# Attention in a decoder layer: which engine copies the spread reciprocals out of PSUM

## The chip, the cores and the metric

The kernel runs on one core of a Trainium2 chip. Five engines work side by side and meet at semaphores: TensorE (PE), VectorE (DVE), ScalarE (ACT), GpSimd (POOL) and SyncE (SP, which issues the DMAs). Each takes its instructions strictly in the order in which they are written. The metric is the device time of one execution in microseconds, median of three runs: 1494.46 us before the change (1493.82 to 1495.74).

## The reference

A pre-norm decoder layer: self-attention, cross-attention and a feed-forward block, each added to x. The change lies in the self-attention, and of it the reference computes:

```python
q = (x @ Wq).reshape(B, T, H, Dh)          # B 4, T 512, H 16, Dh 32
k = (x @ Wk).reshape(B, T, H, Dh)
v = (x @ Wv).reshape(B, T, H, Dh)
scores = jnp.einsum('bthd,bshd->bhts', q, k)
mask = jnp.tril(jnp.ones((T, T), dtype=scores.dtype))
scores = scores * mask
attn = jax.nn.softmax(scores / T ** 0.5, axis=-1)
out = jnp.einsum('bhts,bshd->bthd', attn, v).reshape(B, T, H * Dh)
return out @ Wo
```

The mask multiplies, so tokens beyond the diagonal keep a score of zero and still count in the softmax.

## The kernel before

The four batches (n) are walked one after the other; each has an attention stage of about 62 us, and between two stages stand the projections, the cross-attention and the norms, in which PE is nearly always busy. After the fourth stage comes the feed-forward block (from about 545 us).

An attention stage has 16 units u. A unit is a row tile of 128 queries (i = u % 4, so 128, 256, 384 or 512 tokens wide) of one group of four heads (hg = u // 4); its four rows j are the heads. "Row (u, j)" is the place in the loops that all engines share. In row (u, j):

- PE issues `scores` of the unit after (u+1, j) and then `turn` (u, j), the transposes of the probabilities into a PSUM bank. At j = 3 it also issues `recips(u-1)`, which spreads the reciprocals of a unit's denominators over 32 columns a head by a matmul with the identity, and `values(u-1)`, the product with V. At (4, 1), (8, 1), (12, 1) it issues `repack`, twelve transposes of packed feed-forward weights.
- ACT issues `exp` (u, j), and copies three of the four turned heads to SBUF (`turned`, L1223). At j = 1 it issued `recip_out(u-2)`, L1229: the spread reciprocals from PSUM into `r_den`. At (4, 3), (8, 3), (12, 3) it issues `repacked`, the copy of the first half of the packed weights (L1243).
- DVE works one unit ahead of `exp`: it issues `row_max` (the row maxima, L1548), at j = 3 the copy of the fourth turned head (`turned`, L1558), and at (u, 0), behind its `row_max`, `divide(u-3)`, L1586: the values in bank 6 times `r_den` into `o_sum`. The second half of the packed weights is its copy too (L1599).
- POOL turns each row maximum into the exp's bias (`shift`, L682), masks values (L692), converts packed weights (L675) and for head groups 0 to 2 takes the low part of the output (`out_tail`, L698), which the next group's first `divide` waits for (`o_lo`).

All turned heads, the spread reciprocals and the packed weights go through a ring of three PSUM banks (4, 5, 7). Slot s may be written when slot s-3 has been read, and `turn_read` says who reads that:

```python
def turn_read(n, slot):
    for u in range(UNITS):
        if slot == recip_slot(u):
            return rden_out, n * UNITS + u + 1
```

Three slots behind the spread reciprocals of unit u stands the third turned head of unit u+2 (`turn(u+2, 2)`), for u = 2, 6 and 10 the first half of `repack`, and for u = 14 the spread reciprocals of unit 15. Each has this wait on `rden_out`, the semaphore that the copy into `r_den` raises:

```python
def turn(n, u, j):
    if slot >= 3:
        pe.wait_ge(*turn_read(n, slot - 3))
def repack(n, r):
    for half in range(2):
        pe.wait_ge(*turn_read(n, pack_slot(r, half) - 3))
def recips(n, u):
    pe.wait_ge(*turn_read(n, slot - 3))
```

At the end of a stage ACT and DVE copy the next batch's normed x (L1186, L1533) before the last two units are divided.

Of the kernel before, what the change touches and what calls it, by code (L numbers as in the profile page):

```python
# [46 lines left out]
P = 128  # L47
# [8 lines left out]
UNITS = HG * TT  # L56
# [35 lines left out]
def decoder_layer(nc, x, ctx_1024, Wq, Wk, Wv, Wo, xWq, xbq, xWk, xbk, gate_p, gate_s, up_p, up_s, down_p, down_s, out):  # L92
    with ExitStack() as ctx:
        def sem(name):
            return ctx.enter_context(nc.semaphore(name))
# [26 lines left out]
        def sb(name, shape, dt):  # L122
            return first.enter_context(nc.sbuf_tensor(name, shape, dt))
# [26 lines left out]
        r_den = sb("r_den", [P, 2, P], F32)  # L150
# [87 lines left out]
        pt_act, pt_dve, av_done, o_done, o_hi, o_lo = (sem(n) for n in ("pt_act", "pt_dve", "av_done", "o_done", "o_hi", "o_lo"))  # L238
        den_done, rcol_done, r_full, rden_out = (sem(n) for n in ("den_done", "rcol_done", "r_full", "rden_out"))
# [18 lines left out]
        ROWS = 4 * UNITS  # L258
        wide = [(i + 1) * P for i in range(TT)]

        def turn_slot(h):


            return h + 2 * (max(0, h - 2) // 16) + max(0, h // 4 - 1)

        def pack_slot(r, half):
            return (turn_slot(16 * r + 17) + 1 if r < HG - 1 else recip_slot(UNITS - 2) + 1) + half

        def recip_slot(u):
            return turn_slot(4 * u + 7) + 1 if u < UNITS - 1 else pack_slot(HG - 1, 1) + 1  # L270

        def turn_bank(slot):
            return bank[(4, 5, 7)[slot % 3]]
# [14 lines left out]

        AT_RECIP, AT_DIVIDE = 9, 12
        AT_SUMS, AT_TURNED, AT_RECIPROCALS = 1, 3, 2
        AT_OUT = 0

# [887 lines left out]
        def _(act):  # L1182
            def spread_heads(st, n, banks):
                for k in range(KT):
                    act.wait_ge(spread_full[st], n * KT + k + 1)
                    nc.scalar.activation(spread_to(st, n, 0, k), bank[banks + k][:], ACT.Copy, scale=XF if st == 2 else XS).then_inc(spread_hi[st], 1)  # L1186
# [15 lines left out]
            def exp(n, u, j):  # L1202
                i = u % TT
                act.wait_ge(shift_done, n * ROWS + 4 * u + j + 1)
                if u >= 2:
                    act.wait_ge(t_full, n * ROWS + 4 * (u - 2) + j + 1)
                nc.scalar.activation(prob[:, u % 2, j, 0:wide[i]], bank[j][:, 0:wide[i]], ACT.Exp,  # L1207
                                     bias=nmx[:, u % 2, j:j + 1], accum_out=den[:, u % 2, j:j + 1]).then_inc(exp_done, 1)

            def exp_zero(n, u):  # L1210

                if u >= 2:
                    act.wait_ge(den_done, beyond_units(n, u - 2))
                    act.wait_ge(v_zero_done, beyond_units(n, u - 2))
                act.wait_ge(shift_done, n * ROWS + 4 * u + 4)
                nc.scalar.activation(e_zero[:, u % 2, :], nmx[:, u % 2, :], ACT.Exp).then_inc(e_zero_done, 1)

            def turned(n, u, j):
                i = u % TT
                act.wait_ge(t_full, n * ROWS + 4 * u + j + 1)  # L1220
                if u >= 2:
                    act.wait_ge(av_done, n * UNITS + u - 1)
                nc.scalar.copy(prob_t[:, u % 2, j, 0:wide[i]], turn_bank(turn_slot(4 * u + j))[:, 0:wide[i]]).then_inc(pt_act, 1)  # L1223

            def recip_out(n, u):
                act.wait_ge(r_full, n * UNITS + u + 1)
                if u >= 2:
                    act.wait_ge(o_done, n * UNITS + u - 1)
                nc.scalar.copy(r_den[:, u % 2, :], turn_bank(recip_slot(u))[:, 0:P]).then_inc(rden_out, 1)  # L1229

            def out_head(n, hg):
                act.wait_ge(o_done, n * UNITS + 4 * hg + 4)
                if hg == 0:
                    act.wait_ge(xf_stored, n * 16 + 16)
                nc.scalar.copy(o_t[:, 0, hg, :], o_sum[:]).then_inc(o_hi, 1)

            def repacked(n, r):
                nb = n * (NB // B) + r
                act.wait_ge(pk_full, 2 * nb + 1)
                act.wait_ge(sd_stored, 16 * NB)  # L1240
                if r > 0:
                    act.wait_ge(pk_stored, 32 * nb)
                nc.scalar.copy(pk_t[:, 0], turn_bank(pack_slot(r, 0))[:].bitcast(F16)[:, 0:HALF]).then_inc(pk_out0, 1)  # L1243
# [188 lines left out]
            def body(n, last):  # L1432
                for u in range(UNITS):
                    for j in range(4):
                        if u == 1 and j == 0:
                            act.wait_ge(att_full, n * KT + KT)
                        if u > 0:
                            exp(n, u, j)
                        if j == 3 and u % TT < TT - 1:
                            exp_zero(n, u)  # L1440
                        if j == AT_OUT and u % TT == 2 and u > TT:
                            out_head(n, u // TT - 1)

                        if j >= 2:
                            turned(n, u, j - 2)
                        elif j == 0 and u > 0:
                            turned(n, u - 1, 2)
                        if j == 3 and u % TT == 0 and u > 0:
                            repacked(n, u // TT - 1)
                        h = 4 * u + j - AT_RECIP  # L1450
                        if h >= 0 and h % 4 == 0:
                            recip_out(n, h // 4)
                turned(n, UNITS - 1, 2)
                if not last:
                    spread_heads(0, n + 1, 0)
                for u in range((ROWS - 1 - AT_RECIP) // 4 + 1, UNITS - 1):
                    recip_out(n, u)
                repacked(n, HG - 1)
                recip_out(n, UNITS - 1)
                out_head(n, HG - 1)  # L1460
                between(n, True, not last)

            walk(body)(act)


# [24 lines left out]
        def _(dve):  # L1490
# [87 lines left out]
            def divide(n, u):  # L1578

                hg, i = u // TT, u % TT  # L1580
                if i == 0 and hg > 0:
                    dve.wait_ge(o_hi, n * HG + hg)
                    dve.wait_ge(o_lo, n * HG + hg)
                dve.wait_ge(rden_out, n * UNITS + u + 1)
                dve.wait_ge(av_done, n * UNITS + u + 1)
                nc.vector.scalar_tensor_tensor(o_sum[:, P * i:P * i + P], bank[6][:, P * (u % 2):P * (u % 2) + P], QS, r_den[:, u % 2, :],  # L1586
                                               ALU.mult, ALU.mult).then_inc(o_done, 1)
# [296 lines left out]
            def body(n, last):  # L1884
# [27 lines left out]
                if not last:  # L1912
                    spread_tails(0, n + 1, 0)
                divide(n, UNITS - 2)
                repacked(n, HG - 1)
                divide(n, UNITS - 1)
# [63 lines left out]
```

## Time and profile before

| | us |
|---|---|
| median of 3 runs | 1494.46 |
| lowest, highest | 1493.82, 1495.74 |
| the profiled execution's own time | 1495.65 |
| its span, first to last instruction | 1493.9 |
| busy in the span: PE, DVE, ACT, POOL | 1429.5, 991.0, 723.6, 379.6 |

The span is 1.75 us shorter than the execution's own time. Busy time is summed over stages that have different limits. Instructions of one engine overlap in the rows: one starts while the last still writes, so the start of the next less the start of this is the time that it takes in the queue, and its duration is the time until its result is there. A number in square brackets at the end of a row is the idle time of the engine just before it, with what ended it.

### The profile page before, as it was taken

The page shows a single profiled execution, that of the slowest core. Times are in us where ns is not written, and L with a number is a line of the kernel's source. Part 1 is how long each engine was busy: PE and PEld are TensorE (multiplying, and loading weights), DVE is VectorE, ACT ScalarE, POOL GpSimd, SP SyncE. Part 2 cuts the span into 40 slices and gives each one's busy share as a digit, 9 for nine tenths or more (in the row PEclk, how much of TensorE's full clock was granted, in tenths as well). Part 3 has the DMA queues.
Part 4 walks back from the last instruction along what each step waited for, and adds up shares of the span by engine and source line. Part 5 has one row for each costly group of instructions (what it writes and reads, how often), then busy time and mean ns, then how long its engine had stood idle before and what let it go on. Part 6 is the DMA issues. An engine that isn't in the chain of part 4 may idle for free.

```text
span 1493.9 us, 26821 instructions
## 1 busy us (share of the span) xinstructions
PE 1429.5 (96%) x8896; PEld 722.3 (48%) x8896; DVE 991.0 (66%) x2113; ACT 723.6 (48%) x1676; POOL 379.6 (25%) x688
## 2 busy tenths in 40 slices
PE   6989999999988799999999999999999999999999
PEld 4465456456545554444444444444444444444444
DVE  7785787578567858877666656755766666666533
ACT  5795289249616855353353353343442533533532
POOL 0051024004371865522112111112212212212100
PEclk9999999999999999999999999999999999999999
DMA  7553423341444431011001001001001000000011
GB/s 246 145 154 107 127 75 101 93 117 66 160 138 124 143 112 45 1 32 32 17 17 32 17 17 32 16 17 34 17 16 32 17 16 30 16 20 1 1 57 57
DMA packets 72765, 93.29 MB, mean 62 GB/s; under 512 B 6064, under 2 KB 57008, under 8 KB 72240
## 3 DMA queue, kind: packets, MB, share of 16 engines
q1 hardware_dynamic: 72624, 91.51, 19.9%
q8 instruction: 76, 1.25, 0.3%
q14 instruction: 65, 0.53, 0.1%
HBM read 66.59 MB, written 24.90 MB: 61 GB/s over the span
## 4 chain that ended last, share of the span: by engine, by line
PE 79%; DVE 7%; ACT 6%; issue 6%; POOL 2%; DMA 0%; ACTq 0%; DVEq 0%; POOLq 0%; SPq 0%
PE bank L829 23%; PE bank L830 23%; PE bank L831 23%; ACT prob L1207 3%; PE bank L893 2%; PE bank L914 2%; PE bank L842 1%; PE bank L954 1%; PE bank L969 1%; PE bank L882 1%; ACT prob_t L1223 1%; PE bank L964 1%; PE bank L923 1%; DVE G L1665 1%; DVE c L1690 1%
## 5 line engine op out<-in xcount | busy, mean ns | idle before, releaser
L829 PE MATMUL bank<-xs,G 128*128 128x512 f16 x896 | 339.8, 379 | 2.6 <-ACT c L1295 1.2
L831 PE MATMUL bank<-xs,G 128*128 128x512 f16 x896 | 339.6, 379 | 0.0
L830 PE MATMUL bank<-xs,G 128*128 128x512 f16 x896 | 339.6, 379 | 0.0
L1295 ACT COPY c<-bank 128x512 f32<-128x512 f32 x192 | 111.2, 579 | 219.1 <-PE bank L831 214.3
L1676 DVE TENSOR_TENSOR c<-bank,c 128x512 f32<-128x512 f32 x128 | 88.0, 689 | 192.8 <-PE bank L831 192.8
L829 PE MATMUL bank<-Wd,hid 128*128 128x512 f16 x512 | 194.1, 379 | 2.8 <-DVE X L1730 2.8
L830 PE MATMUL bank<-Wd,hid 128*128 128x512 f16 x512 | 194.0, 379 | 0.0
L831 PE MATMUL bank<-Wd,hid 128*128 128x512 f16 x512 | 194.0, 379 | 0.0
L667 POOL TENSOR_TENSOR c<-c,m 128x512 f32<-128x512 f32 x64 | 82.1, 1284 | 386.3 <-ACT c L1295 386.3
L1730 DVE SCALAR_TENSOR_TENSOR X<-bank,col,X 128x512 f32<-128x512 f32 x128 | 95.4, 749 | 101.5 <-PE bank L831 101.4
L1548 DVE CUSTOM_DVE_ANT_0 bank<-bank,mask,col 128x128 f32<-128x128 f32 (+3 forms) x256 | 139.2, 549 | 26.0 <-issue 13.9
L1207 ACT ACTIVATE prob<-bank,nmx 128x128 f32<-128x128 f32 (+3 forms) x256 | 147.4, 579 | 10.3 <-POOL nmx L682 9.7
L829 PEld LDWEIGHTS bank<-xs,G 128*128 128x128 f16 x896 | 87.6, 98 | 114.9 <-ACT c L1295 7.3
L831 PEld LDWEIGHTS bank<-xs,G 128*128 128x128 f16 x896 | 87.7, 98 | 105.7
L830 PEld LDWEIGHTS bank<-xs,G 128*128 128x128 f16 x896 | 87.7, 98 | 102.5
L682 POOL TENSOR_TENSOR nmx<-zero,mx 128x1 f32<-128x1 f32 x256 | 52.8, 207 | 316.8 <-DVE mx L1548 296.9
L893 PE MATMUL bank<-ident,prob 128*128 128x128 f32 x640 | 112.0, 277 | 16.9 <-DVE prob_t L1558 4.9
L1318 ACT CAST hid<-c 128x512 f16<-128x512 f32 x128 | 79.2, 619 | 91.6 <-DVE c L1690 88.1
L1310 ACT ACTIVATE c<-c,col 128x512 f32<-128x512 f32 x96 | 69.4, 723 | 94.8 <-DVE c L1676 94.8
L1696 DVE TENSOR_TENSOR hid<-c,hid 128x512 f16<-128x512 f32 x128 | 86.1, 712 | 27.0 <-ACT hid L1318 27.0
L633 POOL TENSOR_TENSOR w_sum<-w_full 128x384 f32<-128x384 f32 (+1 forms) x32 | 23.6, 737 | 313.9 <-DVE w_full L1657 313.8
L1223 ACT COPY prob_t<-bank 128x128 f32<-128x128 f32 (+2 forms) x192 | 89.2, 465 | 8.4 <-PE bank L893 8.4
(182 smaller groups left out, 2406.3 us busy)
## 6 DMA issues: line engine op xcount, KB each, us to landing
stack<-qk_dram SPq DMA_DIRECT2D x128, 128.0 KB, 3.3
sc_in<-scale_t SPq DMA_DIRECT2D x32, 384.0 KB
qk_dram<-qk SPq DMA_DIRECT2D x32, 256.0 KB, 2.7
packed_t<-pk_t SPq DMA_DIRECT2D x32, 192.0 KB, 2.0
pk_in<-packed_t SPq DMA_DIRECT2D x32, 192.0 KB
X<-in_x_dram SPq DMA_DIRECT2D x4, 1024.0 KB, 5.8
pk_in<-L_ffn_gate_W_packed_dram SPq DMA_DIRECT2D x16, 256.0 KB, 2.7
pk_in<-n_L_ffn_up_W_packed_dram SPq DMA_DIRECT2D x16, 256.0 KB, 3.0
```

The source lines that it names most:

```text
L667: nc.gpsimd.tensor_tensor(c22[x][:], c22[x][:], m5[x][:], ALU.add).then_inc(c22_out, 1)
L829: pe.matmul(o, lhs(0), rhs(0), start=first, stop=False, skip_group_check=onto)
L830: pe.matmul(o, lhs(0), rhs(1), start=False, stop=False, skip_group_check=onto)
L831: return pe.matmul(o, lhs(1), rhs(0), start=False, stop=stop, skip_group_check=onto)
L893: mm = pe.transpose(turn_bank(slot)[:, P * k:P * k + P], prob[:, u % 2, j, P * k:P * k + P], ident[:])
L1207: nc.scalar.activation(prob[:, u % 2, j, 0:wide[i]], bank[j][:, 0:wide[i]], ACT.Exp, bias=nmx[:, u % 2, j:j + 1], accum_out=den[:, u % 2, ...
L1223: nc.scalar.copy(prob_t[:, u % 2, j, 0:wide[i]], turn_bank(turn_slot(4 * u + j))[:, 0:wide[i]]).then_inc(pt_act, 1)
L1295: nc.scalar.copy(dst[:], bank[BANK_Y if which == M5 else x][:]).then_inc(c_copied, 1)
L1548: nc.vector.tensor_tensor_reduce(out=bank[j][:, 0:wide[i]], in0=bank[j][:, 0:wide[i]], in1=mask[:, P * (3 - i):P * (3 - i) + wide[i]], sca ...
L1676: nc.vector.tensor_tensor(dst[:], bank[at][:], dst[:], ALU.add).then_inc(comb, 1)
L1696: nc.vector.tensor_tensor(hid[:, beta, q, r, 1, :], quarter(1, idx)[:], hid[:, beta, q, r, 0, :], ALU.subtract).then_inc(hid_lo, 1)
L1730: nc.vector.scalar_tensor_tensor(xv, bank[4 + t][:], C_OUT, xv, ALU.mult, ALU.add).then_inc(acc_out, 1)
```

## The change

`recip_out` is taken out of ACT's program. DVE issues the same copy at the head of `divide(n, u)`, behind a wait for `r_full` (the spread reciprocals are in the bank), and raises `rden_out` with it. The multiplication behind it still waits for `rden_out`, now raised by DVE itself.

```diff
-        AT_RECIP, AT_DIVIDE = 9, 12
+        AT_DIVIDE = 12
...
-            def recip_out(n, u):
-                act.wait_ge(r_full, n * UNITS + u + 1)
-                if u >= 2:
-                    act.wait_ge(o_done, n * UNITS + u - 1)
-                nc.scalar.copy(r_den[:, u % 2, :], turn_bank(recip_slot(u))[:, 0:P]).then_inc(rden_out, 1)
...
-                        h = 4 * u + j - AT_RECIP
-                        if h >= 0 and h % 4 == 0:
-                            recip_out(n, h // 4)
...
-                for u in range((ROWS - 1 - AT_RECIP) // 4 + 1, UNITS - 1):
-                    recip_out(n, u)
                 repacked(n, HG - 1)
-                recip_out(n, UNITS - 1)
...
             def divide(n, u):
 
                 hg, i = u // TT, u % TT
+                dve.wait_ge(r_full, n * UNITS + u + 1)
+                nc.vector.tensor_copy(r_den[:, u % 2, :], turn_bank(recip_slot(u))[:, 0:P]).then_inc(rden_out, 1)
                 if i == 0 and hg > 0:
                     dve.wait_ge(o_hi, n * HG + hg)
                     dve.wait_ge(o_lo, n * HG + hg)
                 dve.wait_ge(rden_out, n * UNITS + u + 1)
```

There are 64 such copies, 16 in each attention stage. The instructions of PE, POOL and SP keep their order.

DVE, row (5, 0) of a stage, where the unit divided is 2 and the bank is the one that `repack` takes next. Before:

```order
L1548 ISA bank0,mx<-bank0,mask,col 128x256 [waits shift_done,s_full]
L1548 ISA mx 128x1
L1586 SCALAR_TENSOR_TENSOR o_sum<-bank6,r_den 128x128 [waits av_done,rden_out]
L1599 CAST pk_t<-bank5 128x768 [waits sd_stored,pk_full]
L1548 ISA bank1,mx<-bank1,mask,col 128x256 [waits shift_done,s_full]
```

and now (lines of the changed file):

```order
L1536 ISA bank0,mx<-bank0,mask,col 128x256 [waits shift_done,s_full]
L1536 ISA mx 128x1
L1570 COPY r_den<-bank4 128x128 [waits r_full]
L1576 SCALAR_TENSOR_TENSOR o_sum<-bank6,r_den 128x128 [waits av_done,rden_out]
L1589 CAST pk_t<-bank5 128x768 [waits sd_stored,pk_full]
L1536 ISA bank1,mx<-bank1,mask,col 128x256 [waits shift_done,s_full]
```

The copy stands behind the row maxima of (5, 0), and the multiplication and everything after it one instruction further back. On ACT the same copy stood at row (4, 1), as here before the change:

```order
L1207 ACTIVATE prob,den<-bank1,nmx 128x128 [waits t_full,shift_done]
L1229 COPY r_den<-bank4 128x128 [waits o_done,r_full]
L1207 ACTIVATE prob,den<-bank2,nmx 128x128 [waits t_full,shift_done]
L1223 COPY prob_t<-bank5 128x128 [waits av_done,t_full]
L1207 ACTIVATE prob,den<-bank3,nmx 128x128 [waits t_full,shift_done]
```

It moved from between two exponentials of unit 4 to three rows later in the common order, on the other engine.

PE at rows (4, 0) to (4, 3), the same before and now; bank 4 is the first that `repack` writes:

```order
L882 MATMUL bank0<-stack 128x256 [waits exp_done]
L893 MATMUL bank5<-ident,prob 128x128 [waits pt_act,exp_done]
L882 MATMUL bank1<-stack 128x256 [waits exp_done]
L893 MATMUL bank7<-ident,prob 128x128 [waits pt_dve,exp_done]
L989 MATMUL bank4<-ident16,pk_16 128x128 [waits rden_out,pk_conv]
L989 MATMUL bank4<-ident16,pk_16 128x128 x5
L989 MATMUL bank5<-ident16,pk_16 128x128 [waits pt_act]
L989 MATMUL bank5<-ident16,pk_16 128x128 x5
L882 MATMUL bank2<-stack 128x256 [waits exp_done]
L893 MATMUL bank7<-ident,prob 128x128 [waits pt_act,exp_done]
L882 MATMUL bank3<-stack 128x256 [waits exp_done]
L893 MATMUL bank4<-ident,prob 128x128 [waits pk_out0,exp_done]
```

The first row, into bank 0, is the product whose row maxima DVE takes in row (5, 0). What moved is not PE's order but who raises `rden_out` for its fifth row, and behind what.

## Rows read from the trace of the kernel before

**Rows 1.** Page, its span and part 1: busy us (share) x instructions.

```profile
span 1493.9 us, 26821 instructions
...
PE 1429.5 (96%) x8896; PEld 722.3 (48%) x8896; DVE 991.0 (66%) x2113; ACT 723.6 (48%) x1676; POOL 379.6 (25%) x688
```

**Rows 2.** Windows: length; PE, PEld, DVE, ACT, POOL busy; clock; DMA share; GB/s.

```profile
72.00:134.00 62.00, 55.74 (x824) 40.61 (x825) 48.77 (x187) 57.72 (x205) 26.89 (x97) 1.00 0.52 152
134.00:204.00 70.00, 68.58 (x328) 34.62 (x325) 45.34 (x122) 21.63 (x51) 1.23 (x7) 1.00 0.37 106
...
475.00:545.00 70.00, 56.42 (x806) 39.63 (x807) 53.59 (x194) 56.82 (x200) 47.30 (x116) 0.98 0.44 141
```

**Rows 3.** Groups by line: the copy that moves; busy, mean ns, idle before.

```profile
L1229 ACT COPY r_den<-bank 128x128 f32<-128x128 f32 x64 | 19.6, 306 | 0.4 <-PE bank L923 0.2
```

**Rows 4.** Timeline of ACT, first stage: start us, us, instruction, idle before.

```profile
99.91 0.82 ACT L1243 CAST pk_t<-bank 128x768 int16<-128x768 f16 x1
...
105.91 0.29 ACT L1229 COPY r_den<-bank 128x128 f32<-128x128 f32 x1
106.05 0.63 ACT L1207 ACTIVATE prob<-bank,nmx 128x384 f32<-128x384 f32 x1
...
109.10 0.72 ACT L1207 ACTIVATE prob<-bank,nmx 128x512 f32<-128x512 f32 x1
```

**Rows 5.** Timeline of DVE, first stage, rows (9, 0) to (10, 1).

```profile
99.60 0.29 DVE L1586 SCALAR_TENSOR_TENSOR o_sum<-bank,r_den 128x128 f32<-128x128 f32 x1
100.04 0.56 DVE L1599 CAST pk_t<-bank 128x768 int16<-128x768 f16 x1 [0.16 <-PE bank L989]
...
101.86 0.29 DVE L1558 COPY prob_t<-bank 128x128 f32<-128x128 f32 x1
...
103.40 0.29 DVE L1586 SCALAR_TENSOR_TENSOR o_sum<-bank,r_den 128x128 f32<-128x128 f32 x1
103.60 0.62 DVE L1548 CUSTOM_DVE_ANT_0 bank<-bank,mask,col 128x384 f32<-128x384 f32 x1
```

**Rows 6.** Timeline of DVE in a norm: each waits for the one before.

```profile
422.00 0.46 DVE L1516 SCALAR_TENSOR_TENSOR rs<-rs,var 128x4 f32<-128x4 f32 x1
422.49 0.17 DVE L1518 SCALAR_TENSOR_TENSOR rs<-rs 128x4 f32<-128x4 f32 x1
```

**Rows 7.** Timeline of PE, first stage: the second repack, and three turned heads that wait.

```profile
99.17 0.83 PE L989 MATMUL bank<-ident,pk 128*128 128x128 f16 x12
...
100.87 0.30 PE L893 MATMUL bank<-ident,prob 128*128 128x128 f32 x1 [0.29 <-ACT pk_t L1243]
...
103.27 0.38 PE L893 MATMUL bank<-ident,prob 128*128 128x128 f32 x2
...
110.84 0.63 PE L893 MATMUL bank<-ident,prob 128*128 128x128 f32 x4 [0.64 <-ACT prob L1207]
```

**Rows 8.** Timeline of POOL, units 10 and 11 of the first stage.

```profile
104.35 0.44 POOL L682 TENSOR_TENSOR nmx<-zero,mx 128x1 f32<-128x1 f32 x1 [0.55 <-DVE mx L1548]
...
106.51 1.16 POOL L698 TENSOR_TENSOR o_t<-o_sum,o_t 128x512 f16<-128x512 f32 x1
...
108.88 0.19 POOL L682 TENSOR_TENSOR nmx<-zero,mx 128x1 f32<-128x1 f32 x1 [1.07 <-DVE mx L1548]
```

**Rows 9.** Timeline of DVE, unit 11 of the first stage.

```profile
107.75 0.29 DVE L1586 SCALAR_TENSOR_TENSOR o_sum<-bank,r_den 128x128 f32<-128x128 f32 x1 [0.81 <-issue]
...
110.14 0.55 DVE L1558 COPY prob_t<-bank 128x384 f32<-128x384 f32 x1
```

**Rows 10.** Timeline of DVE, end of the first stage.

```profile
131.78 0.28 DVE L1586 SCALAR_TENSOR_TENSOR o_sum<-bank,r_den 128x128 f32<-128x128 f32 x1
```

**Rows 11.** Timeline of PE, end of the first stage.

```profile
132.21 1.08 PE L914 MATMUL bank<-prob_t,V 128*32 128x128 f32 x32 [0.69 <-DVE o_sum L1586]
```

**Rows 12.** Timeline of DVE in the last stage.

```profile
480.38 0.36 DVE L1640 TENSOR_SCALAR bits<-pk_in 128x384 uint32<-128x384 uint32 x1 [1.37 <-DMA sc_in<-scale_t]
```

**Rows 13.** Timeline of POOL in the last stage.

```profile
487.12 1.66 POOL L622 TENSOR_TENSOR w_full<-codes,sc_in 128x768 f32<-128x768 f16 x1
```

## The prediction

> **What bounds the kernel now.** I read the page first, then the busy time by stage, then the groups by line, and last the timelines of all engines side by side through one period of four units. The page gives PE 1429.5 us of a span of 1493.9 [rows 1], so the kernel is bound by PE as a whole; but the change touches the four attention stages alone, and there it looks otherwise. In a window of 62 us over the first stage ACT is busy 57.72 us, PE 55.74, DVE 48.77; the 70 us behind it have PE at 68.58 and ACT at 21.63 [rows 2]. So ACT is the fullest engine in attention, and whatever delay PE leaves a stage with is not made up behind it. The last stage carries feed-forward work too: DVE 53.59 and ACT 56.82 of 70 us [rows 2].
>
> The copy that moves takes 19.6 us in 64 pieces, 306 ns each [rows 3]. Its price in ACT's queue is smaller: it starts at 105.91 and the next exponential at 106.05, 0.14 us [rows 4].
>
> **What is removed.** 64 x 0.14 = 9.0 us of ACT's queue, 2.2 us a stage. It is worth time only where ACT is what the others wait for.
>
> **What is added on DVE.** The trace has a DVE copy of this very size out of PSUM: 0.29 us [rows 5]. The multiplication behind it now waits for its result. In a norm, where each instruction waits for the one before, one of 0.46 us starts at 422.00 and the next at 422.49, 0.03 us after its end [rows 6]. So each copy pushes what is behind it on DVE by 0.29 + 0.03 = 0.32 us: 20.5 us in all, 5.1 a stage, against 62 - 48.8 = 13.2 us in which DVE is free. Ends: 0.20, the time in the queue of a multiplication of this size with no wait behind it (103.40 to 103.60 [rows 5]), and 0.46, the longest small instruction of rows 6. I take 0.32.
>
> The multiplication that nothing waits behind lets the next start 0.09 us before its own end [rows 5], the one that is waited for 0.03 us after its end [rows 6]: the wait costs 0.12 us. The Trainium skill, "VectorE: DVE Perf Modes", section "The DRAIN you can't avoid", says of chained copies that a semaphore after each costs nothing extra. By that rule the copy would cost 0.20 and the sum below would be 17 x 0.12 = 2.0 us less; the rows here say otherwise.
>
> **What the later copy holds up.** This is the part that the diff does not show. `rden_out` does not only release the multiplication; it also frees the bank that PE writes three slots later. Before, ACT read it at row (u+2, 1). Now DVE reads it at row (u+3, 0), behind the row maxima of the unit u+3, and these wait for scores that PE issues only just ahead of the instruction that needs the bank.
>
> For u = 2, 6, 10 that instruction is the first transpose of `repack`. In the second period it starts at 99.17 [rows 7], with DVE's multiplication at 99.60 [rows 5]. The copy takes that place, ends at 99.89, and PE goes on 0.15 us after DVE's end (DVE's copy starts at 110.14 and takes 0.55, PE starts at 110.84 [rows 7, 9]): 100.04. The bank is 0.87 us late. Behind it queue on PE the rest of the repack, the scores of (9, 2) and (9, 3), the turned heads, the spread and the values; on ACT the copy of packed weights, at 99.91 [rows 4]; on DVE the other, at 100.04, which already waited for PE by 0.16 [rows 5]. PE's turned head (8, 3) already waited 0.29 for ACT's copy [rows 7]. The first half of a repack takes about 0.5 us of the 0.83, so ACT's copy had some 0.2 us to spare. That leaves 0.65 us of each, three times a stage. Ends: 0 (all absorbed) and 0.87.
>
> In the other units it is a transpose (u+2, 2). For u = 7 DVE's multiplication stands at 103.40 and PE's transpose (9, 2) at 103.27 [rows 5, 7]: 103.40 + 0.29 + 0.15 = 103.84, 0.57 us late, and much the same where u % 4 is 0. But PE waits for ACT soon after, and the copies of turned heads on ACT come later still; I take nothing. For u % 4 = 1 the copy stands in front of the wait below. Ends: 0, and 0.5 us for each of 8 a stage.
>
> **Where 0.32 us lies on the path.** From row (10, 0) on, DVE works without a gap into the row maxima that POOL waits for: 104.35, idle 0.55 for DVE. POOL then runs through to the low part of the output, 106.51 plus 1.16 us, and DVE stands 0.81 us until it is done and divides at 107.75 [rows 8, 9]. From there DVE runs through again; POOL waits for its maximum, 108.88 plus 0.19, and ACT's exponential starts at 109.10, 0.03 us after it; PE's transpose at 110.84 starts 0.15 us after DVE's copy ends [rows 4, 7, 8, 9]. So DVE, POOL, DVE is a chain with no slack, as long as ACT's own. The copy at row (10, 0) lengthens it by 0.32. The copy at (11, 0) does not: it stands in front of the 0.81 us of waiting. This chain is there in rows (6, 0), (10, 0) and (14, 0) to (u+1, 0): three times a stage. At the end of a stage DVE copies the normed x, divides at 131.78, and PE, idle 0.69 us, starts the last values 0.15 us after it, at 132.21 [rows 10, 11]; the copy adds 0.32 in front.
>
> **The sum.** A stage: 3 x 0.65 + 3 x 0.32 + 0.32 = 3.2 us. Where DVE's chain is as long as ACT's, ACT's gain is lost in waiting; in the first four units, without that chain, two copies are saved: 2 x 0.14 = 0.3. That makes 2.9 us, and 8.8 in three stages. In the last stage DVE is behind a DMA until 480.38 and runs without a gap until POOL starts the weights at 487.12 [rows 12, 13], with two copies in between, 0.64; after that POOL leads for a while. Three more copies are on the chain, 0.96, and one of the three repacks is late by 0.7 with nothing to absorb it; the others wait for ACT or POOL anyway. The end of that stage has no normed x and hides its copy. Together 2.3. In all 8.8 + 2.3 = 11.1 us. On the profiled execution's own 1495.65 us that makes 1506.8; the median of the runs is 1.2 lower, so I predict 1505.6.
>
> **Rivals.**
> *ACT's relief wins.* ACT is the fullest engine [rows 2], DVE has the room, and 0.14 us leave ACT 64 times: 9.0 us, 1485.5. It needs all DVE delays to fall into DVE's gaps and PE to get its banks in time; the transpose at 110.84 and the exponential at 109.10 speak against it [rows 4, 7], since both follow DVE. The Trainium skill, "Perfetto Trace Analysis", section "Optimizing Scalar/DVE Operations", says that work may be moved between the two when one is saturated, which read this way round speaks for the change; it also gives DVE the larger access overhead on PSUM, which agrees with 0.20 against 0.14 us in the queue [rows 4, 5].
> *DVE's time alone.* The late bank is absorbed by the waits of 0.29 and 0.16 us and by ACT's queue. A stage: 0.96 + 0.32 - 0.3 = 1.0; the last 1.6; in all 4.6: 1499.1.
> *All of it hides*, gain and loss cancel: 1494.5.
> *The late transposes count too.* From the point where the three-bank ring is the limit, nothing absorbs them: 8 a stage at up to 0.5 us, some 3 us a stage net, 12 more than the forecast: 1518.
>
> **How the numbers follow.** A change under 0.2%, 3 us, cannot be told from none by a measurement of this kernel. Chances: forecast 0.57, DVE's time alone 0.15, late transposes 0.12, all hides 0.08, ACT's relief 0.08. The two bounds of the copy (0.20 and 0.46) move the sum by -2.0 and +2.4 us over its 17 places, the ends of the repack term move it by -6.5 and +2.2 over its ten. The range that holds 8 in 10 goes from 1498, with the case of DVE's time alone, to 1513. Faster 0.08, same 0.09, slower 0.83.
>
> **What would show it.** In the profile after: the DVE copy into `r_den` at 0.28 to 0.30 us and the multiplication 0.03 us behind it; before each `repack` PE idle by 0.5 us or more, put down to DVE; the periods from one repack to the next longer by about 1.0 us; the DVE busy time up by 18 us, ACT's down by 20. The stretches between the attention stages and the feed-forward block keep their length. I am wrong if PE does not wait at the repack, if the copy stands in a gap of DVE in the rows (u, 0) with u % 4 = 2, or if the attention stages grow shorter.

## The result: 0.6% slower, and the profile after

The changed kernel takes 1503.80 us (median of 4 runs, 1502.88 to 1506.35), the kernel before 1494.93 us (4 runs on the same chip). The ratio is 1.0062, with a 95% interval from 1.0046 to 1.0077, so the loss of 8.9 us is real. The profiled execution of the changed kernel took 1503.5 us, against 1495.65 before.

The page of the kernel after, its span and part 1, which answer to [rows 1]:

```profile
span 1501.8 us, 26765 instructions
...
PE 1428.0 (95%) x8896; PEld 720.2 (48%) x8896; DVE 1003.7 (67%) x2177; ACT 718.1 (48%) x1612; POOL 379.0 (25%) x688
```

PE does the same work in the same time; the span is 7.9 us longer, and all of this is idle PE. The windows of the kernel after say where (length; busy of PE, PEld, DVE, ACT, POOL; clock; DMA share; GB/s), the same first two stretches as [rows 2]:

```profile
72.00:134.00 62.00, 53.32 (x780) 38.66 (x780) 50.33 (x198) 55.99 (x188) 26.88 (x98) 1.00 0.51 150
134.00:204.00 70.00, 68.39 (x357) 34.77 (x358) 45.18 (x121) 20.14 (x44) 0.76 (x4) 1.00 0.38 111
```

In 62 us of the first attention stage PE is busy 2.4 us less than before, and ACT, which lost its copies, is now idle for 6.0 us instead of 4.3. Nobody was waiting for the time that ACT was given.

The groups by line of the kernel after (busy, mean ns of one, idle before them and its releasers): the copy in its new place, and the first repack instructions.

```profile
L1570 DVE COPY r_den<-bank 128x128 f32<-128x128 f32 x64 | 18.3, 286 | 0.0
...
L989 PE MATMUL bank<-ident,pk 128*128 128x128 f16 x192 | 13.7, 219 | 8.7 <-DVE r_den L1570 7.6 <-ACT prob_t L1223 1.2
```

PE waits 7.6 us at the repacks for the copy that DVE now makes. The list of waits of the kernel after (engine, line, releaser: us in all, times, longest) counts them, and shows the other place:

```profile
PE bank L989 <- DVE r_den L1570: 7.6, 11, 0.7
...
PE bank L923 <- DVE r_den L1570: 2.9, 3, 1.0
```

Eleven repacks of the twelve with u = 2, 6, 10 wait, and the three stages that end in a norm wait once more at their end. One such repack on all engines, second period of the first stage, timelines of the kernel after (start us, us, instruction, idle before). It answers to [rows 4, 5, 7]. DVE:

```profile
100.23 0.14 DVE L1536 DVE_READ_ACCUMULATOR2_ANT mx<- 128x1 f32 x1
100.23 0.29 DVE L1570 COPY r_den<-bank 128x128 f32<-128x128 f32 x1
100.55 0.29 DVE L1576 SCALAR_TENSOR_TENSOR o_sum<-bank,r_den 128x128 f32<-128x128 f32 x1
101.53 0.56 DVE L1589 CAST pk_t<-bank 128x768 int16<-128x768 f16 x1 [0.69 <-PE bank L989]
```

PE, and behind it ACT:

```profile
100.66 0.83 PE L989 MATMUL bank<-ident,pk 128*128 128x128 f16 x12 [0.70 <-DVE r_den L1570]
```

```profile
101.19 0.80 ACT L1237 CAST pk_t<-bank 128x768 int16<-128x768 f16 x1 [0.54 <-PE bank L989]
```

The copy ends at 100.52 and PE starts 0.14 us later, after 0.70 us of idling. ACT then waits 0.54 us for PE, and DVE 0.69 instead of 0.16: the lateness of one 0.29 us instruction reaches three engines.

Starts of the first repack instruction in the first stage: 84.05, 99.17, 114.29, 130.31 before; 84.61, 100.66, 116.72, 132.92 after. A period of four units, 15.12 us before, takes 16.05. The last values of the stage move from 132.21 [rows 11] to 135.14, those of the second stage from 264.17 to 270.02, those of the third from 396.09 to 404.87: 2.93, 2.92 and 2.93 us a stage.

### The profile page after: what moved, and what is told of

It is laid out like the page before. It is cut to its first block, busy times and chain, and to the rows that moved or that the text cites. A ratio compares the mean times of both kernels' runs of the same rounds, so it can differ in the third digit from the quotient of the medians.

```text
span 1501.8 us, 26765 instructions
## 1 busy us (share of the span) xinstructions
PE 1428.0 (95%) x8896; PEld 720.2 (48%) x8896; DVE 1003.7 (67%) x2177; ACT 718.1 (48%) x1612; POOL 379.0 (25%) x688
## 3 DMA queue, kind: packets, MB, share of 16 engines
q8 instruction: 76, 1.25, 0.4%
## 4 chain that ended last, share of the span: by engine, by line
PE 81%; issue 7%; DVE 5%; ACT 3%; POOL 3%; DMA 0%; POOLq 0%; ACTq 0%; DVEq 0%; SPq 0%
PE bank L829 24%; PE bank L831 24%; PE bank L830 24%; PE bank L893 2%; ACT prob L1207 2%; PE bank L914 2%; POOL nmx L682 1%; PE bank L842 1%; PE bank L954 1%; PE bank L969 1%; PE bank L964 1%; POOL pk L675 1%; PE bank L882 1%; ACT prob_t L1223 1%; POOL v_zero L692 1%
## 5 line engine op out<-in xcount | busy, mean ns | idle before, releaser
L1536 DVE CUSTOM_DVE_ANT_0 bank<-bank,mask,col 128x128 f32<-128x128 f32 (+3 forms) x256 | 139.2, 550 | 21.2 <-issue 13.2
L1207 ACT ACTIVATE prob<-bank,nmx 128x128 f32<-128x128 f32 (+3 forms) x256 | 140.2, 557 | 15.6 <-POOL nmx L682 13.4
L893 PEld LDWEIGHTS bank<-ident,prob 128*128 128x128 f32 x640 | 74.4, 140 | 50.9 <-ACT prob L1207 25.6
```

The source lines that it names most:

```text
L893: mm = pe.transpose(turn_bank(slot)[:, P * k:P * k + P], prob[:, u % 2, j, P * k:P * k + P], ident[:])
L1536: nc.vector.tensor_tensor_reduce(out=bank[j][:, 0:wide[i]], in0=bank[j][:, 0:wide[i]], in1=mask[:, P * (3 - i):P * (3 - i) + wide[i]], sca ...
```

## The experiments

All times are medians; each ratio is to the kernel before, run on the same chip (its median there was 1495.28 us beside early_all, early_u2, early_u3 and no_copy, 1495.54 beside dve_only, bank_only and early_act_tail, 1496.10 beside act_late and early_act_tail_2). "Period" is the distance from the second repack of the first stage to the third, and "three stages" how much later (or earlier) than before the last values of the third stage start.

| kernel | us | ratio, 95% interval | period us | three stages us |
|---|---|---|---|---|
| before | 1494.93 | 1 | 15.12 | 0 |
| after | 1503.80 | 1.0062, 1.0046 to 1.0077 | 16.06 | +8.78 |
| early_all | 1494.76 | 0.9997, 0.9988 to 1.0007 | 15.09 | -0.51 |
| early_u2 | 1498.72 | 1.0020, 1.0010 to 1.0030 | 15.42 | +3.23 |
| early_u3 | 1501.46 | 1.0038, 1.0024 to 1.0052 | 15.74 | +5.76 |
| no_copy | 1493.76 | 0.9995, 0.9985 to 1.0004 | 15.10 | -0.70 |
| dve_only | 1499.08 | 1.0030, 1.0018 to 1.0041 | 15.42 | +3.35 |
| bank_only | 1501.56 | 1.0038, 1.0024 to 1.0052 | 15.76 | +6.59 |
| early_act_tail | 1494.01 | 0.9987, 0.9978 to 0.9997 | 15.10 | -1.79 |
| early_act_tail_2 | 1494.69 | 0.9993, 0.9984 to 1.0002 | 15.12 | -1.25 |
| act_late | 1544.23 | 1.0326, 1.0310 to 1.0342 | 18.46 | +38.2 |

### The copy on DVE, but in time: early_all, early_u2, early_u3

The edit to the changed kernel (early_all; the others have `(2,)` and `(3,)` in place of the four numbers). The last two lines stand ahead of the row maxima of row (u, 0) in DVE's loop:

```
+            def recip_out(n, u):
+                dve.wait_ge(r_full, n * UNITS + u + 1)
+                nc.vector.tensor_copy(r_den[:, u % 2, :], ...).then_inc(rden_out, 1)
             def divide(n, u):
-                dve.wait_ge(r_full, n * UNITS + u + 1)
-                nc.vector.tensor_copy(...).then_inc(rden_out, 1)
+                if not (u <= UNITS - 4 and u % TT in (0, 1, 2, 3)):
+                    recip_out(n, u)
...
+                        if j == 0 and u >= 3 and (u - 3) % TT in (0, 1, 2, 3):
+                            recip_out(n, u - 3)
```

> DVE's copies of units 0 to 12 stand ahead of the row maxima of row (u+3, 0) instead of behind them; those of the last three units of a stage stay at the division. Late bank and serial DVE time as causes: PE gets the bank of the repack back before it asks for it (no wait on DVE's copy there), the copies at rows (6, 0), (10, 0), (14, 0) fall into DVE's wait for PE's scores, and only the 0.32 us at the end of three stages is left, against 0.28 us won in their first four units. 1494 to 1496 us, periods between repacks 15.1 us again. If instead the total of DVE's work (18 us more) were the cause, the time would stay at about 1503.

Measured 1494.76 us, ratio 0.9997: with the copy ahead of the row maxima nothing of the loss is left, although DVE does as much as in the changed kernel (1002.5 us busy against 1003.7). PE, first stage of early_all:

```profile
98.26 0.83 PE L989 MATMUL bank<-ident,pk 128*128 128x128 f16 x12
113.35 0.83 PE L989 MATMUL bank<-ident,pk 128*128 128x128 f16 x12
```

No idle time stands at either repack. What cost 8.9 us is the place of the copy in DVE's order, not the engine. The copies of the last three units of a stage are not moved here, and their price is still there: PE waits 0.96 us for DVE's copy at the end of the third stage, and of the 0.85 us by which the repack ahead of it is early (393.35 against 394.20) 0.51 is left at the last values (395.58 against 396.09).

> Only the copies of units 2, 6 and 10 go ahead of the row maxima, all others stay as in the changed kernel. This takes away the late bank alone. Late bank worth 0.6 to 0.65 us at each of nine repacks of three stages and one or two of the last: a period falls from 16.06 to about 15.45 us, the time from 1503.8 to about 1497. If the late bank is absorbed and DVE's serial time is the cause: no change from 1503.8.

Measured 1498.72 us, 1.7 above the expectation, with the rival at 1503.8 ruled out. PE, first stage of early_u2:

```profile
99.40 0.83 PE L989 MATMUL bank<-ident,pk 128*128 128x128 f16 x12
114.82 0.83 PE L989 MATMUL bank<-ident,pk 128*128 128x128 f16 x12
```

The period is 15.42 against 16.06: the late bank of one unit in four costs 0.64 us. Over three stages it is 8.78 - 3.23 = 5.55 us, on average 0.62 for each of nine repacks.

> Only the copies of units 3, 7 and 11 go ahead of the row maxima, where DVE waits for PE's scores anyway. This takes 0.32 us out of the chain DVE, POOL, DVE alone and leaves the bank of the repack late. Periods of 16.06 us fall to about 15.74, the time from 1503.8 to about 1500.5. If the bank alone is the cause: 1503.8.

Measured 1501.46 us. PE, first stage of early_u3:

```profile
100.30 0.83 PE L989 MATMUL bank<-ident,pk 128*128 128x128 f16 x12 [0.70 <-DVE r_den L1568]
116.04 0.83 PE L989 MATMUL bank<-ident,pk 128*128 128x128 f16 x12 [0.70 <-DVE r_den L1568]
```

The wait of 0.70 us is as in the changed kernel, and the period is 0.32 us shorter: the copy in front of row (10, 0) is taken out of the chain from DVE to POOL and back. Three stages: 8.78 - 5.76 = 3.02 us, nine times 0.34. The two terms add up: 15.10 + 0.64 + 0.32 = 16.06.

### What ACT's relief is worth: no_copy

Nobody copies; DVE multiplies by the identity matrix instead of by the spread reciprocals, so the output is not divided by the sums.

```
-                    return rden_out, n * UNITS + u + 1
+                    return r_full, n * UNITS + u + 1
...
-                nc.vector.scalar_tensor_tensor(..., QS, r_den[:, u % 2, :],
+                nc.vector.scalar_tensor_tensor(..., QS, ident[:],
```

> Neither engine copies: the multiplication takes the identity matrix in place of the reciprocals, and their bank counts as free as soon as PE has written it. So the softmax is not divided by its sum. This is ACT's relief alone, with no cost on DVE and no late bank. If ACT's queue set the pace of the attention stages, 64 x 0.14 = 9.0 us: 1485.5 us. If the chain over DVE and POOL is as long as ACT's, as I think: 0.3 to 0.6 us a stage, 1492 to 1494 us.

Measured 1493.76 us, ratio 0.9995 (0.9985 to 1.0004), as the theory said; the rival's 1485.5 is far outside. PE, first stage of no_copy, repacks in the rhythm of [rows 7]:

```profile
99.18 0.83 PE L989 MATMUL bank<-ident,pk 128*128 128x128 f16 x12
114.28 0.83 PE L989 MATMUL bank<-ident,pk 128*128 128x128 f16 x12
```

ACT is spared 4 x 0.14 = 0.56 us of its queue in a period (its busy time there falls by 0.40, from 14.54 to 14.14) and the period shrinks by 0.02. The fullest engine of the stage was not the one that set its length.

### Each cost by itself, in the kernel before: dve_only, bank_only

dve_only leaves ACT's copy where it is and lets DVE make a second one, of PE's result, ahead of the multiplication, and wait for it:

```
+                if i > 0 and u < UNITS - 1:
+                    dve.wait_ge(av_done, n * UNITS + u + 1)
+                    nc.vector.tensor_copy(o_sum[:, P * i:P * i + P], bank[6][...]).then_inc(spare_done, 1)
+                    dve.wait_ge(spare_done, n * 11 + u - u // TT)
```

> The kernel before, with a copy of the same size added on DVE at each division with u % 4 not 0 except that of unit 15 (values from PSUM into the part of o_sum that the division then overwrites), and a wait for it. ACT still copies the reciprocals and frees their bank. This is DVE's serial time alone. 0.32 us three times a stage on the chain over POOL and once at the end: 1.3 us in each of three stages, about 1 in the last: 1494.9 + 5 = 1500, periods of 15.12 us going to 15.44. If only the late bank matters: 1495.

bank_only adds no work. PE waits, before it writes a bank that held spread reciprocals, for DVE's division of that unit as well (for u % 4 = 0, for the row maximum ahead of it):

```
+        def turn_free(eng, n, slot):
+            eng.wait_ge(*turn_read(n, slot))
+            for u in range(UNITS):
+                if slot == recip_slot(u) and u % TT == 0:
+                    eng.wait_ge(max_done, n * ROWS + 4 * (u + 3) + 1)
+                elif slot == recip_slot(u) and u < UNITS - 1:
+                    eng.wait_ge(o_done, n * UNITS + u + 1)
...
-                    pe.wait_ge(*turn_read(n, slot - 3))
+                    turn_free(pe, n, slot - 3)
```

> The kernel before, with one wait more on PE: the bank of the spread reciprocals of unit u counts as free only when DVE's division of u is done (where u % 4 is 0: when the row maximum of row (u+3, 0) is done). That is the moment at which the copy ends in the changed kernel, 99.89 us in the second period; ACT still copies, and DVE has no more work. This is the late bank alone: 0.55 to 0.65 us at each of nine repacks in three stages and one or two in the last, 5 to 6 us: about 1500.5. If only DVE's time matters: 1495.

Measured: dve_only 1499.08 us (+3.5 on the 1495.54 of before on that chip), bank_only 1501.56 (+6.0). PE, first stage of dve_only and of bank_only:

```profile
98.74 0.83 PE L990 MATMUL bank<-ident,pk 128*128 128x128 f16 x12
114.16 0.83 PE L990 MATMUL bank<-ident,pk 128*128 128x128 f16 x12
```

```profile
100.84 0.83 PE L998 MATMUL bank<-ident,pk 128*128 128x128 f16 x12 [0.70 <-DVE o_sum L1595]
116.60 0.83 PE L998 MATMUL bank<-ident,pk 128*128 128x128 f16 x12 [0.70 <-DVE o_sum L1595]
```

The extra instruction lengthens the period by 0.30 us without a wait of PE, the late bank by 0.64 us with the same 0.70 us of waiting as in the changed kernel, though no instruction was added at all. Together they make 9.5 us, where the change costs 8.9; neither of them has the 0.3 us a stage that the changed kernel saves in its first four units (below).

### The engine or the place: act_late

ACT still copies, two rows later in its own order, and for that the lines of the copy stand ahead of the packed weights in its loop; DVE does not copy.

```
-        AT_RECIP, AT_DIVIDE = 9, 12
+        AT_RECIP, AT_DIVIDE = 11, 12
...
+                        h = 4 * u + j - AT_RECIP
+                        if h >= 0 and h % 4 == 0:
+                            recip_out(n, h // 4)
                         if j == 3 and u % TT == 0 and u > 0:
                             repacked(n, u // TT - 1)
```

> The kernel before, with ACT still making the copy, but two rows later in ACT's own order: at row (u+2, 3), behind the turned probabilities of that row, instead of at row (u+2, 1). DVE does not copy at all. My theory says that the price of a late bank has nothing to do with which engine reads it: for u = 2, 6, 10 the copy then starts where ACT's last turned copy ahead of the packed weights ends, about 99.9 in the second period of the trace of before, so that the repack may start at about 99.9 + 0.29 + 0.15 = 100.3 instead of 99.17, and with 0.2 us to spare the period grows from 15.12 to about 16.0 (15.8 to 16.3), the three stages by 2.5 to 3.5 us each, and the whole to about 1504 (1501 to 1508); PE should stand idle before the repack for ACT. The rival, that it is DVE's own time and its wait that cost (the copy in DVE's queue), says that DVE is untouched here and the period stays at 15.12, the time at 1495.5.

Measured 1544.23 us, ratio 1.0326. Both expectations missed: the rival had 1495.5, and mine had the right sign and 40 us too little. PE in the second period of act_late:

```profile
86.74 0.83 PE L989 MATMUL bank<-ident,pk 128*128 128x128 f16 x12 [1.00 <-ACT r_den L1229]
...
91.77 0.41 PE L893 MATMUL bank<-ident,prob 128*128 128x128 f32 x2 [1.00 <-ACT r_den L1229]
...
96.32 0.52 PE L893 MATMUL bank<-ident,prob 128*128 128x128 f32 x3 [0.95 <-ACT r_den L1229]
...
101.29 0.63 PE L893 MATMUL bank<-ident,prob 128*128 128x128 f32 x4 [1.14 <-ACT r_den L1229]
...
105.19 0.83 PE L989 MATMUL bank<-ident,pk 128*128 128x128 f16 x12 [1.00 <-ACT r_den L1229]
```

PE waits in all four units, about 1.0 us each, and the period grows by 3.3 us. I had put a price on the repack alone and let the other three units be absorbed, as in the changed kernel. The list of waits of act_late:

```profile
DVE o_sum L1586 <- ACT r_den L1229: 61.7, 55, 1.9
PE bank L893 <- ACT r_den L1229: 43.1, 40, 1.4
PE bank L989 <- ACT r_den L1229: 13.2, 12, 2.2
```

43.1 + 13.2 = 56.3 us of PE's idle time are named after the copy, and the kernel is 48 us slower. As I read the order of the instructions, the copy stands behind turned probabilities that PE must first have transposed, so each engine waits for the other in turn, and slack elsewhere does not help; no run here tests this reading. It is the rival of the late transposes, in another kernel than the one for which I had weighed it. DVE's multiplication waits for the same copy (61.7 us), and this run does not separate that wait from the one for the bank. What it does show is that a late place costs time with ACT as the reader too, although DVE does nothing more than before.

### A version that keeps both: early_act_tail, early_act_tail_2

early_all, with the copies of the last three units of a stage made by ACT, where DVE is busy with the norm:

```
+            def recip_out(n, u):
+                act.wait_ge(r_full, n * UNITS + u + 1)
+                act.wait_ge(rden_out, n * UNITS + u)
+                act.wait_ge(o_done, n * UNITS + u - 1)
+                nc.scalar.copy(r_den[:, u % 2, :], ...).then_inc(rden_out, 1)
...
+                        if u == UNITS - 1 and j == 1:
+                            recip_out(n, UNITS - 3)
...
+                recip_out(n, UNITS - 2)
                 repacked(n, HG - 1)
+                recip_out(n, UNITS - 1)
```

> As the kernel with all early copies on DVE, but the copies of units 13, 14 and 15 of each stage are ACT's again. This takes the 0.32 us at the end of three stages away too: about 1 us less than with all copies on DVE, 1493 to 1495 us, so at best a little faster than the kernel before. If the end of the stage is not bound by DVE's copy: the same time as with all copies early.

> A second measurement of the kernel whose first thirteen copies of a stage are made by DVE ahead of the row maxima and the last three by ACT: the first gave 0.9987 of the time before, with an interval from 0.9978 to 0.9997, at the edge of what can be told from no change. If the gain is real the ratio comes out at 0.998 to 0.9995 again, about 1494.0 against 1495.3; the rival, that it was chance, says 1.000. The trace should show the same stages as before: periods of 15.10 and the first stage ended 1.3 to 1.4 us earlier than in the kernel before.

Measured 1494.01 us, ratio 0.9987 (0.9978 to 0.9997), and on another chip 1494.69, ratio 0.9993 (0.9984 to 1.0002). It beats the changed kernel by 9 us or a little more, as early_all does. Against the kernel before it is 1 to 2 us faster by the medians; the second interval holds 1, so a gain is likely but not shown. The first stage does end 1.36 us earlier. PE, last values of the first stage of early_act_tail, against [rows 11]:

```profile
130.85 1.08 PE L914 MATMUL bank<-prob_t,V 128*32 128x128 f32 x32 [0.70 <-DVE o_sum L1588]
```

Most of that is the start: the first repack stands at 82.75 instead of 84.05. How much of it is the edit's is not shown, for that start moves by itself: in dve_only, which only adds work, it is at 83.33. Further on the gain does not add up with each stage (1.36, 1.77, 1.79 us after one, two, three), and 0.3 us is left of it in the feed-forward block. The second trace has periods of 15.12 us and is 0.97 us early at the last repack of the first stage (129.34 against 130.31), less than I had expected of it.

## Why the prediction was right, and where a size was off

**What bounds the stages.** Right: not ACT, though it is the fullest, but a chain from DVE through POOL and PE. no_copy shows it from the side of ACT (0.02 us a period for 0.56 us of work), dve_only from the side of DVE (0.30 us for one copy).

**The copy and its wait, 0.32 us.** Right to the hundredth: 100.23 to 100.55 in the rows above. The multiplication starts 0.03 us behind the copy's end, as forecast. The wait alone makes 0.12 of it, since a multiplication that nothing waits for lets the next start after 0.20 [rows 5], and so does this very copy where nothing waits for it. DVE in early_all:

```profile
105.23 0.28 DVE L1568 COPY r_den<-bank 128x128 f32<-128x128 f32 x1
105.43 0.75 DVE L1536 CUSTOM_DVE_ANT_0 bank<-bank,mask,col 128x512 f32<-128x512 f32 x1
```

The rule of the Trainium skill ("VectorE: DVE Perf Modes", section "The DRAIN you can't avoid"), that a semaphore between chained operations costs nothing extra, does not hold in these traces: 0.32 us with the wait, 0.20 without.

**The late bank, 0.65 us net for each repack.** Right. PE's last instruction ahead of the second repack, kernel before and kernel after:

```profile
99.06 0.27 PE L893 MATMUL bank<-ident,prob 128*128 128x128 f32 x1
```

```profile
99.69 0.27 PE L893 MATMUL bank<-ident,prob 128*128 128x128 f32 x1
```

The repack started 0.11 us behind it [rows 7] and now starts 0.97 behind it, at 100.66. So it is late by 0.86 us (forecast 0.87); the 0.70 in brackets is less, because the transpose ahead of it is still running for a part of that time. 0.64 stays in the period, so 0.22 is absorbed (forecast 0.2).

The late transposes were absorbed, as forecast. Turned head (9, 2), kernel after:

```profile
105.09 0.41 PE L893 MATMUL bank<-ident,prob 128*128 128x128 f32 x2 [0.40 <-ACT prob L1207]
```

The row names ACT, but PE starts 0.14 us after the end of DVE's copy (104.66 and 0.29), just as at the repack. It costs nothing all the same: early_u2 keeps the late transposes and dve_only has none, and both have periods of 15.42 us. (The prediction calls the unit whose copy stands in front of the wait for POOL u % 4 = 1; it is u % 4 = 0, as its own row (11, 0) says. Nothing in its sum hangs on that.) act_late suggests that the absorption ends where the copy itself stands behind PE.

**The chain through POOL, 0.32 us three times.** Right. The POOL and DVE rows of unit 11, kernel after, against [rows 8, 9]:

```profile
108.10 1.16 POOL L698 TENSOR_TENSOR o_t<-o_sum,o_t 128x512 f16<-128x512 f32 x1
...
110.47 0.19 POOL L682 TENSOR_TENSOR nmx<-zero,mx 128x1 f32<-128x1 f32 x1 [1.07 <-DVE mx L1536]
```

```profile
108.39 0.29 DVE L1570 COPY r_den<-bank 128x128 f32<-128x128 f32 x1
109.34 0.29 DVE L1576 SCALAR_TENSOR_TENSOR o_sum<-bank,r_den 128x128 f32<-128x128 f32 x1 [0.67 <-POOL o_t L698]
```

The copy at row (11, 0), that of unit 8, stands in front of the wait for POOL, as forecast, and adds nothing there. From POOL's output at 108.10 to its next wait, 1.07 us at 110.47, everything is as before, 1.59 us later.

**The end of a stage, 0.32 us.** Right. DVE copies at 134.39 behind the normed x, and PE, kernel after, waits for that copy instead of for the multiplication, from the repack (132.92) to the values 2.22 us instead of 1.90:

```profile
134.72 0.43 PE L923 MATMUL bank<-ident,r_col 128*32 128x128 f32 x8 [0.96 <-DVE r_den L1570]
135.14 1.08 PE L914 MATMUL bank<-prob_t,V 128*32 128x128 f32 x32
```

The sum for a stage was 2.9 us and the stages grew by 2.93, 2.92 and 2.93. Piece by piece it was less exact: the first repack came 0.56 us later (0.35 by the terms), the next two periods gave 0.93 and 0.94 (0.97), the fourth 0.18 (0.32). The other kernels show why. A repack's delay is absorbed only behind it, so the first one shows its 0.86 whole and the fourth period gives 0.22 back (16.20 us, where early_u2 has 16.42). The 0.3 us saved in the first four units is there too: from the last values of the first stage to the first repack of the second it takes 83.76 us before, 84.30 in the changed kernel, 83.46 in no_copy and 83.44 in early_all and early_u2.

**The last stage, 2.3 us: the term that was mis-sized.** It added 0.64 in the two traces. Its first part was right. DVE and POOL there, kernel after, against [rows 12, 13]:

```profile
488.04 0.36 DVE L1630 TENSOR_SCALAR bits<-pk_in 128x384 uint32<-128x384 uint32 x1 [1.09 <-DMA sc_in<-scale_t]
```

```profile
495.43 1.66 POOL L622 TENSOR_TENSOR w_full<-codes,sc_in 128x768 f32<-128x768 f16 x1
```

The distance between them was 6.74 and is 7.39 us, 0.65 more, where 0.64 was forecast for two copies. The other kernels bear it out: 7.07 in dve_only, which has one such copy there, 6.75 in bank_only, which has none, and 7.14 in early_all, where nothing waits for the two (0.20 each). But DVE waits for a DMA there, and that wait ended 7.66 us later than before while PE entered the stage 7.92 late, so 0.26 came back. Then POOL leads. I had 1.66 us more behind it, for three copies and one late repack; of these 0.25 was left at the end of the stage (543.59 to 552.15 for the last values, 8.56). The late repack is there, and not once but twice (at 497.84 PE idles 0.70 us for the copy, and a turned head at 489.41 waits 1.59 us for one). PE of the kernel after:

```profile
517.93 0.90 PE L989 MATMUL bank<-ident,pk 128*128 128x128 f16 x12 [0.57 <-DVE r_den L1570]
...
520.21 1.91 PE L914 MATMUL bank<-prob_t,V 128*32 128x128 f32 x32
```

It is 9.04 us later than before, 0.73 more than POOL was. How the rest was absorbed is not settled, because the clock moved as well (below). From the first matmul on `xw_t` ahead of it (450.94 before) to its last values the kernel before takes 92.65 us and the kernel after 93.29, dve_only 92.77 and bank_only 92.44. But early_all takes 93.18, and early_u3 and early_u2, which have less to pay than the changed kernel, 93.97 and 94.29 (in both the clock falls twice, below). So 0.64 is no more than this stretch differs by for other reasons, and from one trace of each kernel its price can't be told more closely. The medians say that it is small: in each of the kernels that lose time, act_late aside, the whole loss is within 0.6 us of what the three stages show (8.9 against 8.78 in the changed kernel, 3.5 against 3.35 in dve_only, 6.0 against 6.59 in bank_only, 3.4 against 3.23 in early_u2, 6.2 against 5.76 in early_u3). In that stage neither cost is on the path for long.

**Between the stages.** I had said that these stretches keep their length, and from the third stage to the cross attention behind it (396.09 to 450.94 before, 404.87 to 458.86 after) the changed kernel took 0.86 us less. No edit explains it: the same stretch takes 54.38 us in dve_only, 55.56 in bank_only, 55.36 in early_u2, 56.07 in early_u3 and 55.77 in early_act_tail, against 54.85 and 53.99. It varies by 2 us for its own reasons (below). The feed-forward block gave back 0.7 us more, in four steps of 0.25 to 0.34 and one of 0.47 the other way: 8.56 us late at its start, 8.31 from 769 us (in the kernel before), 7.98 from 998, 8.45 from 1035, 8.18 from 1113, 7.84 from 1342 to its end. This block too differs without an edit to it: from the last values of the fourth stage to the end of the span it takes 950.3 us before and 949.7 after, 949.2 in early_all and 950.9 in bank_only. What makes the steps is not settled.

**The sum.** 8.8 + 2.3 = 11.1 us were forecast, and in the two traces it is 8.78 + 0.64 - 0.86 - 0.7 = 7.9 us; by the medians 8.9. The three stages carry all of it. The term that was too large is the one for the last stage; the two stretches that were to keep their length took back 1.6 us, which is as much as such stretches differ without an edit.

**Busy times.** Forecast DVE +18, ACT -20 us; measured +12.7 and -5.5. I had taken the sum of the durations, and busy time counts rows that lie over each other once. In the second period of the first stage DVE's busy time rises from 12.12 to 13.04 us, 0.23 for each of four copies of 0.29: the copy of unit 8, for one, starts at 108.39 together with the 0.14 us read of the accumulator and adds only the rest. In no_copy, where ACT's copies are gone and nothing else is late, its busy time falls by 8.0 us, 0.12 a copy, near the 0.14 of [rows 4]; why it falls by only 5.5 in the changed kernel is not settled. The mechanism was argued with the place in the queue, so nothing hung on it, but as a check it was badly posed.

## What to carry to other kernels

Before a copy out of PSUM is moved to another engine, ask who writes that bank next, and where the copy comes to stand in the new engine's order against work that waits for that writer; here the place cost 0.64 us a period, the instruction 0.32, and the relief of the fullest engine was worth 0.02. Busy shares do not tell which engine sets the period: a chain through DVE (79% busy in the first stage), POOL (43%) and PE (90%) did, while ACT at 93% did not. If work is moved onto such an engine, put it ahead of the instruction that waits longest there: with 52 of the 64 copies in such a place nothing of the loss was left.

## What the runs showed of the hardware

- A DVE instruction that the next one waits for on the same engine costs 0.12 us more than its place in the queue: 0.32 against 0.20 us for 128x128 f32, in the changed kernel (100.23 to 100.55) and in dve_only (99.17 to 99.49, then 99.70 behind the multiplication); the copy that nothing waits for takes 0.20 in early_all (105.23 to 105.43).
- In the last stage the granted clock of TensorE fell to its lower level (half) for a few us, in the kernel before and in the kernel after at different places; the 32 value matmuls that came under it took 1.93 and 1.91 us instead of 1.06. Windows of the kernel before, and of the kernel after, around the fall:

```profile
524.00:527.00 3.00, 1.63 (x34) 1.01 (x22) 0.76 (x4) 1.19 (x7) 2.67 (x6) 1.00 0.43 139
527.00:530.00 3.00, 2.54 (x34) 1.79 (x38) 2.11 (x10) 2.93 (x13) 1.27 (x5) 0.68 0.25 93
```

```profile
515.00:518.00 3.00, 0.65 (x4) 0.33 (x5) 2.97 (x11) 1.62 (x9) 1.56 (x5) 1.00 0.02 7
518.00:521.00 3.00, 3.00 (x40) 2.29 (x43) 2.24 (x10) 1.68 (x5) 2.25 (x3) 0.59 0.23 82
```

  Before, the clock fell around the third repack of the stage; after, around the second, where PE had worked 0.65 of 3.00 us ahead of it (1.11 in the like stretch before, from 506 to 509, where the clock stayed at 1.00). Each of these two kernels pays once, at another place, and that hides how much of the repack's delay was absorbed. early_u2, early_u3 and both traces of early_act_tail pay twice.
- The same happens in front of the cross attention. After 4.73 us without work PE turns the normed x at the lower level (granted clock 0.50 from 426 to 432 us in the kernel before; in the kernel after 0.66 from 436 to 438 and 0.50 to 440). PE, kernel before and kernel after:

```profile
427.91 3.68 PE L842 MATMUL bank<-ident,xn 128*128 128x128 f32 x16 [4.73 <-DVE xn L1521]
```

```profile
436.38 3.48 PE L842 MATMUL bank<-ident,xn 128*128 128x128 f32 x16 [4.42 <-DVE xn L1509]
```

  16 transposes take 1.91 us at the full clock (128.11 before, 130.72 after). The gap ahead of them is 4.42 to 5.49 us in the eleven traces, and it is part of the 2 us by which that stretch varies; what sets its length in one execution is not settled.
- DVE's wait for the scales of the packed weights ended 7.66 us later than before where PE was 7.92 late. That such a wait takes back part of a loss is likely but not shown: from the first matmul on `xw_t` to its end it is 29.44 us before and 29.18 after, but 28.64 to 29.62 in the other kernels.
